# One expert's layer-1 weights copied per tile instead of its whole record, layer 2 addressed by a register of TensorE, seven places for returning rows, half 1's scatters in two of three steps

## The reference, cut to what matters

```python
def step(state, bc):                     # 512 in a row, state 64 wide
    b_t, c_t = bc
    s = _layernorm(state @ A_bar + b_t, ln_st_g, ln_st_b)
    return (s, c_t * s)
...
logits = xn @ moe_gate_w + moe_gate_b
topw, topi = jax.lax.top_k(logits, K)    # 2 of 8 experts for each token
topw = jax.nn.softmax(topw, axis=-1)
...
h  = _gelu(jnp.einsum('bsd,edh->ebsh', xn, ew1) + eb1[:, None, None, :])   # layer 1: 128 -> 256
eo = jnp.einsum('ebsh,ehd->ebsd', h, ew2) + eb2[:, None, None, :]          # layer 2: 256 -> 128
moe_out = jnp.einsum('ebsd,bse->bsd', eo, w_dense)
for i in range(NROT):
    moe_out = moe_out @ expm(gens[i])
...
x = x + s * g
```

## Time and profile before

| | us |
|---|---|
| runs, median of 3 | 410.24 (409.66 to 414.73) |
| the profiled execution | 405.85, its span 404.0 |
| PE busy in the span | 327.0 (81%) |
| DVE busy | 284.0 (70%) |
| ACT busy | 195.2 (48%) |
| POOL busy | 188.8 (47%) |
| DMA moved | 54.81 MB, 136 GB/s |

### The profile page before, as it was taken

One profiled execution on the slowest core, in us unless ns is written; L12 is line 12 of the kernel. 1 busy time (PEld: TensorE's weight loads), 2 busy tenths in 40 slices (PEclk: granted clock), 3 DMA queues, 4 the chain that ended last, 5 costly groups with the idle time before them and its releaser, 6 DMA issues.

```text
span 404.0 us, 11723 instructions
## 1 busy us (share of the span) xinstructions
PE 327.0 (81%) x4029; PEld 244.4 (60%) x4029; DVE 284.0 (70%) x1357; ACT 195.2 (48%) x587; POOL 188.8 (47%) x261
## 2 busy tenths in 40 slices
PE   2897983997787569996997999999997989887670
PEld 1676941775564347875865877877866765443340
DVE  2547589869877547876553666689999567799970
ACT  1217730201322326673636676587775573587510
POOL 8408950725546437777777545345544251000110
PEclk9999986799989959999898999899999899999955
DMA  8199950411110345665564668866656222600001
GB/s 255 22 190 163 135 117 0 130 35 36 41 40 29 140 123 187 231 222 184 189 195 158 219 192 261 280 215 203 210 178 219 79 92 56 228 28 27 28 29 55
DMA packets 44158, 54.81 MB, mean 136 GB/s; under 512 B 6840, under 2 KB 28767, under 8 KB 44095
## 3 DMA queue, kind: packets, MB, share of 16 engines
q1 hardware_dynamic: 38975, 42.52, 37.7%
q0 software_dynamic: 4544, 9.39, 7.1%
q10 hardware_dynamic: 576, 2.10, 1.5%
HBM read 14.15 MB, written 16.63 MB: 76 GB/s over the span
## 4 chain that ended last, share of the span: by engine, by line
PE 40%; DVE 32%; POOL 8%; issue 8%; DMA 6%; ACT 2%; SPq 2%; POOLq 0%; DVEq 0%; ACTq 0%
PE bank L1478 8%; PE bank L1047 7%; PE bank L1488 5%; DVE wT L949 4%; DVE ring L961 3%; DVE roots L914 3%; DMA token_rows<-rows_out,token_rows_i 3%; DVE sqj L938 2%; PE bank L465 2%; PE bank L492 2%; POOL sorted_rows L1701 2%; POOL late L307 2%; DVE xpad L1254 2%; DVE Rho L916 2%; PE bank L1471 2%
## 5 line engine op out<-in xcount | busy, mean ns | idle before, releaser
L1715 POOL DMA_INDIRECT token_rows<-rows_out,token_rows_i x78 | 75.8, 972 | 71.9 <-ACT rows_out L1612 47.6
L1701 POOL DMA_INDIRECT sorted_rows<-late,slots x64 | 63.8, 997 | 56.6 <-PE bank L1047 34.3
L1047 PE MATMUL bank<-Mrep,wT 32*32 32x64 f32 x2368 | 65.9, 226 | 18.8 <-DVE wT L949 18.0
L1047 PEld LDWEIGHTS bank<-Mrep,wT 32*32 32x32 f32 x2368 | 42.2, 108 | 52.6 <-issue 49.3
L1605 ACT ACTIVATE desk<-bank,record 128x128 f32<-128x128 f32 x156 | 48.9, 366 | 36.1 <-PE bank L1478 35.6
L961 DVE SCALAR_TENSOR_TENSOR ring<-bank,Rho,Dv 128x64 f32<-128x64 f32 x112 | 31.6, 282 | 40.5 <-PE bank L1047 38.6
L1478 PE MATMUL bank<-desk,record 128*128 128x128 f32 x312 | 58.5, 313 | 0.0
L1488 PE MATMUL bank<-record,desk 128*128 128x129 f32 x312 | 50.2, 285 | 0.0
L1478 PEld LDWEIGHTS bank<-desk,record 128*128 128x128 f32 x312 | 43.1, 200 | 7.5 <-issue 1.0
L1488 PEld LDWEIGHTS bank<-record,desk 128*128 128x128 f32 x312 | 43.2, 201 | 0.1
L1597 ACT ACTIVATE desk<-bank,cols 128x128 f32<-128x128 f32 x78 | 36.0, 462 | 6.4 <-PE bank L1471 6.4
(11 more groups left out here) (328 smaller groups left out, 658.8 us busy)
## 6 DMA issues: line engine op xcount, KB each, us to landing
record<-experts SPq DMA_DIRECT2D x78, 290.5 KB
sorted_rows<-zero_rows SPq DMA_DIRECT2D x2, 2515.5 KB, 26.6
desk<-sorted_rows SPq DMA_DIRECT2D x26, 193.5 KB
pulls<-token_rows SPq DMA_DIRECT2D x8, 516.0 KB, 5.2
X<-in_L_attn_x ACTq DMA_DIRECT2D x4, 512.0 KB, 5.5
out<-xT SPq DMA_DIRECT2D x8, 256.0 KB, 2.0
token_rows<-rows_out,token_rows_i POOLq DMA_INDIRECT x78
experts<-in_L_ffn_ew SPq DMA_DIRECT2D x1, 1024.0 KB, 28.1
```

The lines of the kernel that those rows point to most:

```text
L1047: t = pe.matmul(psY[q], wT[q, 32 * c:32 * c + 32], Mrep[q, c, :], start=(c == 0), stop=(c == 1))
L1701: pool.indirect_dma_start(sorted_rows[h], bass.IndirectOffsetOnAxis(ap=slots[:, j, q:q + 1], axis=0), sort_rows[:, q, :], None)\
L1715: pool.indirect_dma_start(token_rows[h], bass.IndirectOffsetOnAxis(ap=token_rows_i[:, g:g + 1], axis=0), rows_out[:, g % OUT_PLACES, :], N ...
```

## The change

The buffers of whole records become `first_w`, five buffers of layer 1's 256 floats a partition (`FIRSTS` = 5), free again when `layer1` of five tiles before is done. Layer 2's weights and its bias are no longer copied: PE reads the tile's expert number into a register itself (`expert_now`, at the end of the slot before) and its three layer-2 operands are addressed in `experts` by it. Layer 1's bias comes from `tile_bias`, which one matmul with a one-hot table makes for all tiles at t = 13 (two more parts of `tile_tables` on DVE at t = 10 and 11, one ACT copy); a transpose and a copy in the front are gone. SP no longer waits for the bias part; PE does, before slot 3. `rows_out` has 7 places. From t = 24 on a scatter stands only in steps that three doesn't divide.

```diff
-RECORDS = 5
-OUT_PLACES = 5
+FIRSTS = 5
+OUT_PLACES = 7
@@ tile_tables
+            elif part == 10:
+                dve.tensor_scalar(one_expert[:, 2, :], expert_f[0:E * K, :, :].rearrange("p h t -> p (h t)"), float(K), slot_at[0:E * K, 0, 0:1],
+                                  ALU.mult, ALU.subtract).then_inc(sem("tables"), 1)
+            elif part == 11:
+                dve.wait_ge(sem("tables"), 11)
+                for k in range(K):
+                    t = dve.tensor_scalar(one_expert[:, k, :], one_expert[:, 2, :], float(-k), None, ALU.is_equal)
+                t.then_inc(sem("tables"), 1)
@@ the tables of steps
+        SCATTER_AT = {}
+        for t in range(STEPS):
+            if SCATTER_LEAD + len(SCATTER_AT) < 4 * Q and (t < 2 * Q - SCATTER_LEAD or t % 3):
+                SCATTER_AT[t] = SCATTER_LEAD + len(SCATTER_AT)
@@ TensorE
+                def expert_now(g):
+                    expert[g] = pe.value_load(expert_of[0:1, g:g + 1], min_val=0, max_val=E - 1)
+
                 def layer1(g):
-                    w, _, _, _ = record_of(g)
-                    pe.wait_ge(sem(f"record{g % RECORDS}"), 16 * (g // RECORDS + 1))
+                    w = first_w[:, g % FIRSTS]
+                    pe.wait_ge(sem(f"first_w{g % FIRSTS}"), 16 * (g // FIRSTS + 1))
...
                 def layer2(g):
-                    _, w, _, bias = record_of(g)
+                    _, w, _, bias = fields(experts[:, ds(expert.pop(g), 1), :].squeeze(1))
...
                     if t in SLOT_AT:
                         j = SLOT_AT[t]
+                        if j == 2:
+                            expert_now(0)
+                        if j == 3:
+                            pe.wait_ge(sem("eb2_stored"), 32)
+                            pe.wait_ge(sem("ew2r_ready"), E)
...
                         if j >= 3:
                             layer2(j - 3)
+                        if 2 <= j < TILES + 1:
+                            expert_now(j - 1)
@@ GpSimd
-                    if SCATTER_LEAD + t < 4 * Q:
+                    if t in SCATTER_AT:
                         pool.wait_ge(sem("product"), turn)
-                        scatter(SCATTER_LEAD + t)
+                        scatter(SCATTER_AT[t])
@@ SyncE
-                    if g >= RECORDS:
-                        sp.wait_ge(sem("rows_done"), g - RECORDS + 1)
-                    sp.dma_start(record[:, g % RECORDS], experts[:, ds(e, 1), :].squeeze(1)).then_inc(sem(f"record{g % RECORDS}"), 16)
+                    if g >= FIRSTS:
+                        sp.wait_ge(sem("pre_hidden"), g - FIRSTS + 1)
+                    sp.dma_start(first_w[:, g % FIRSTS], experts[:, ds(e, 1), 0:F].squeeze(1)).then_inc(sem(f"first_w{g % FIRSTS}"), 16)
...
                 sp.wait_ge(sem("ew1_loaded"), 16)
-                sp.wait_ge(sem("ew2r_ready"), E)
-                sp.wait_ge(sem("eb2_stored"), 32)
```

More of the change, by code:

```diff
@@ L219, in build @@
         mean, var, r1, rz, nm1, nmz, tmp, tmp2 = (lnv[:, i, :] for i in range(8))
-        records = record[:, :, :].rearrange("p a r -> p (a r)")
-        lg, oh1, oh2, rest = (records[:, i * NS * E:(i + 1) * NS * E].rearrange("p (q e) -> p q e", e=E) for i in range(4))
-        hits, places = (records[:, i * NS * E:(i + 2) * NS * E].rearrange("p (e j q) -> p e j q", e=E, j=2) for i in (4, 6))
+        lg, oh1, oh2, rest = (scratch[:, i * NS * E:(i + 1) * NS * E].rearrange("p (q e) -> p q e", e=E) for i in range(4))
+        hits, places = (scratch[:, i * NS * E:(i + 2) * NS * E].rearrange("p (e j q) -> p e j q", e=E, j=2) for i in (4, 6))
         counts = sb("counts", [P, 4, HALVES, E])
@@ L1181, in out_bank @@
             return banks[3 + g % 2][:, 0:W]
-        def record_of(g):
-            return fields(record[:, g % RECORDS])
         def value_steps(n):
@@ L1520, in _ @@
                         ew2_rotation(EW2_ROT_AT[t] + 1)
+                    if t == TILE_BIAS_AT:
+                        pe.wait_ge(sem("tables"), 12)
+                        pe.matmul(banks[5][:, 0:K * TILES], eb1_rows[:, :], one_expert[:, 0:K, :].rearrange("p k t -> p (k t)"), start=True, stop=True)\
+                          .then_inc(sem("tables"), 1)
                     if t == EB2_AT:
+                        pe.wait_ge(sem("tile_bias"), 1)
                         pe.matmul(banks[5][0:E, 0:W], eb2T[:, :], Rall[:, :], start=True, stop=True).then_inc(sem("eb2_rotated"), 1)
@@ L1599, in gelus @@
                 def gelus(g):
-                    _, _, bias, _ = record_of(g)
                     act.wait_ge(sem("pre_hidden"), g + 1)
+                    if g == 0:
+                        act.wait_ge(sem("tile_bias"), 1)
                     if g >= 2:
@@ L1604, in gelus @@
                     for k in range(K):
-                        t = act.activation(hidden[:, g % 2, k, :], hidden_bank(g)[:, k * P:(k + 1) * P], ACT.Gelu, bias=bias[:, k:k + 1])
+                        t = act.activation(hidden[:, g % 2, k, :], hidden_bank(g)[:, k * P:(k + 1) * P], ACT.Gelu, bias=tile_bias[:, k, g:g + 1])
                     t.then_inc(sem("hidden"), 1)
@@ L1625, in _ @@
                         rotated_copy(EW2_ROT_AT[t] + 1)
+                    if t == TILE_BIAS_AT:
+                        act.wait_ge(sem("tables"), 13)
+                        act.copy(tile_bias[:, :, :], banks[5][:, 0:K * TILES].rearrange("p (k t) -> p k t", k=K)).then_inc(sem("tile_bias"), 1)
                     if t == EB2_AT:
@@ L1783, in _ @@
                 for g in range(TILES):
-                    if g + RECORDS < TILES:
-                        fetch(g + RECORDS)
+                    if g + FIRSTS < TILES:
+                        fetch(g + FIRSTS)
                     if g % CHUNK == 0 and g // CHUNK + 3 < TILES // CHUNK:
```

17 lines of the change are left out of this document (10 added, 7 removed).

## The result

The changed kernel takes 418.54 us in the median of 4 runs (416.94 to 421.14), the kernel before beside it 409.95 us (405.63 to 414.73). The ratio is 1.029, its 95% interval 1.024 to 1.035 (it leaves disturbed runs out, so it is not quite the quotient of the medians). So the change makes the kernel **slower by about 3%**. The forecast of 413.0 us was 5.5 us too low. The time lies inside the range of 404 to 422, but beyond the "within 2%" to which I had given the largest chance.

What follows compares the result with a forecast made beforehand. POOL was taken as the bound of the stage from 153.5 to 211.0 us. Gate -1.0 (start included), clock +2.0 and registers +2.0 sum to +3.0 us; shifted onto the median of 410.24 this gives 413, range 404 to 422.

Steps and rivals of the forecast that it cites:

- the time of the gate: Step 73: last scatter starts at 227.8, layer 1 of tile 36 at 233.6, 1.0 us earlier than before (-3.5 to +3).
- Before step 73 POOL hides it all: Slots ahead of step 73: PE's register work costs nothing there, being hidden behind POOL.
- POOL's 60 operations: From the first `rows_back` at 150.6 to the last scatter: 60 x 1.278 = 76.7 us, plus gaps, ending at 227.8.
- 0.5 us of gaps: POOL ahead of the last scatter: idle time before its lag has built up, 0.5 us in all.
- rival 3: Gate at step 73 opens later (slow landing, POOL idling or late fetches): 4 to 6 us more, 417 to 420; chance 0.13.
- The start: Front of the kernel: SP starts 1.5 us earlier without the bias wait; the first rows come 1.4 us earlier in sum.
- The clock: Steps after the stall at step 73: PE at a lower clock costs 2.0 us (bounds 0.5 and 3).
- The registers: Some 40 slots behind step 73: PE's register work for layer 2 costs 2.0 us (bounds 0 and about 8).
- short by about 0.1: Steady slot step on PE: 1.1 us of added sequencer time against 1.14 us of room, some 0.1 for waits.
- Copies of 128 KB: Weight fetches of 128 KB instead of 290.5: no wait there is for a record, so fewer bytes alone save nothing.
- The first (scatters early enough): Step 73: POOL at 1.16 us an operation, so no stall; 403, down to 399 us; chance 0.10.
- The second (register work dear): Slot steps: tight ones short by 0.5, 40 steps at 0.3 more, 12 us: 425, times 418 to 430; chance 0.20.

Runs made afterwards that it cites:

- fixed address: The changed kernel without PE's register read, layer 2 reading expert g modulo 8 at a fixed address (wrong expert for most tiles): 411.46 us, ratio 1.013.
- whole records: The kernel before with seven places and half 1's scatters in two of three steps, copies still of 290.5 KB: 412.71 us, ratio 1.013.

## Why the prediction was right or wrong

**The mechanism and the place were right.** POOL was the bound from 153 us on. The change sets one stall at step 73, for the fetched weights, with all engines standing, and the chain through scatter, load and fetch is as foretold. ACT's waits are gone. The direction was right; the size was 5.5 us short in the median and 12 in the profiled execution.

**The step that failed most is the time of the gate, and in it "Before step 73 POOL hides it all"**. The prediction has "layer 1 of tile 36 starts at 233.6"; it started at 241.57. Behind the last scatter the sum was right to 0.1 us: foretold 227.8 to 233.6, 5.8 us, measured 235.70 to 241.57, 5.87 (landing 2.37 for 2.4, spacing 1.18 for 1.4, the fetch 2.25 for 2.0). The 7.9 us lie ahead of it, in two terms.

- *POOL's 60 operations*: 77.2 us foretold, 155.26 to 235.70, 80.4, measured. The rate was right, 0.30 us of gap behind an operation of 0.96, but "0.5 us of gaps" was 3.2 short. Two waits right behind the first `rows_back` are POOL idling before its lag has built up, as rival 3 had it. The largest gap is at a round's boundary; kernel after:

```profile
198.45 0.96 POOL L1732 DMA_INDIRECT sorted_rows<-late,slots  x1 [2.82 <-PE bank L1055]
```

  and the same place in the kernel without the register, with the same schedule:

```profile
187.54 0.99 POOL L1732 DMA_INDIRECT sorted_rows<-late,slots  x1 [0.16 <-issue]
```

  A scatter waits for its step's product, and a boundary step takes over 4 us. With register work POOL had caught up by then and stood 2.8 us. Without it, in both kernels with this schedule (fixed address, and whole records), POOL has lag enough to ride over the boundary, and the 60 operations take 78.9 and 78.4 us. The likely reason is the pace ahead of it: steps 28 to 50 take 42.3 us after, 40.7 and 40.2 in those two. So of the 3.2 us some 1.6 to 2.0 are the register work, which the prediction held to be hidden ahead of the gate, and the rest are the first waits. It is read from one profile of each kernel.

- *The start*: first `rows_back` at 150.6 foretold, 155.26 measured. As a term of the change it was right. In the run without register whose front is that of before, SP's first read comes 1.48 us earlier (foretold 1.5), and in the three profiled runs with that front steps 0 to 27 take 57.1 to 57.5 us against 58.8 before. The first `rows_back` of one of them, the fixed-address kernel, starts at 151.07, close to the foretold 150.6. The profiled run of after differs in two things that other kernels share: its step 0 starts 1.3 us later, and its steps 20 to 25 run into half clock at 126 to 136 us (15.38 us instead of 11.92), most of which the stall at step 27 gives back (4.2 instead of 7.1 us). Seven places alone on the kernel before has both too. So I count this part of the 12 us as the profiled runs' difference; that no part of it is the change's isn't shown, with one profile of each kernel. It is also why a sum against one execution can't be better than some 4 us here.

**The clock** after the stall: 2.0 us foretold, the shift grows from 7.0 at the gate to 8.9 at step 76, 1.8. The rows of the first stall were the right measure. The half-clock stretch is from 238.9 to 245.7 us. A last one near 380 us cost 1.7 more, which I had not in the sum; runs of other kernels have it in some cases and not in others.

**The registers** were mis-sized: 2.0 foretold, all of it behind the stall, with bounds of 0 and 8, and 6.5 measured by the ratios. Behind the stall the changed kernel's trace has 4.7 us more than before, but not all of it is register work: 2.8 lie in the 36 steps from 76 to 114 that run at full clock in both traces, and 1.9 in three steps that a half-clock stretch touches, which is twice as long after as before. Windows of step starts over these two stretches, after and then before:

```profile
262.80:269.60 6.80, 0.49 (x2) 0.50 0.89 294
...
254.00:257.40 3.40, 0.49 (x2) 0.50 1.00 361
```

The other 1.6 to 2.0 us of register work stand ahead of the gate, as said. The kind of argument was right, an excess over the room of 1.14 us. The failing number was "short by about 0.1": it is 0.3, as one slot of after shows: ACT's copy ends at 224.50, and the next step's first weight load is 1.46 us on, 0.48 of it waiting for issue.

```profile
225.96 0.29 PEld L1055 LDWEIGHTS bank<-Mrep,wT 32*32 32x32 f32 x16 [0.48 <-issue]
```

I had put the three address instructions at 0.09 us each with their gaps; they come 0.13 us apart, and they stand ahead of the matmuls that should cover the read. The read itself, of PE in the kernel after (min, median, max in ns):

```profile
L1486 PEldq TENSOR_LOAD <-expert_of x78: 297/306/570, 149.2 to 343.9; - x78
```

Its median of 0.306 us lies near SP's 0.274 and not at PE's single 0.488 of the earlier trace rows. The Trainium skill's page "DMA: Bandwidth & Descriptors" (latency and other measured facts) gives a `tensor_load` about 600 ns at least; these 78 disagree, and with its figure the forecast would have been nearer the time for a wrong reason.

**Copies of 128 KB**: "fewer bytes save nothing by themselves" held for the stall (9.4 us with whole records, 8.9 and 7.0 with layer 1 alone) and at step 67. Between two of the experiments some 0.8% is unexplained (above), and may be theirs; with the two-in-three schedule nothing is.

**The rivals.** The first (scatters early enough) did not come. The second (register work dear) came in part. The third (a later gate) came, by POOL's gaps and not by the landings that I had named for it. I gave them 0.20 and 0.13 as if apart, but part of the later gate is the register work itself. As large as they came, each alone stays within 2%, and both together pass it. The chance of "slower", 0.28, should have been nearer a half, since my own sum lay at +3 and every open term pointed upward.

## What to carry to other kernels

When a queue is the bound, count its operations up to the one that a later engine waits for, not those per step: thinning them out relieves the steps and makes the last one late. More buffers are the cheap cure for a backlog that ends by itself; starting the queue's work earlier won as much. A wait that hides other work hides it only while it lasts: here the register work cost 1.6% beside the stall and 2.9% without it, and it delayed the very operation that was to hide it. Register work on TensorE's sequencer cost little up to what the queued matmuls cover and then, in this kernel, up to 0.41 of each 0.65 us added, so measure the room first. Here it was cheaper behind the largest group of queued matmuls than ahead of a transpose on which ACT waits.

## What the hardware showed that I had not expected

- The cost of sequencer work on PE isn't proportional: in the profiled runs 0.15 us more (the read alone) costs nothing, the next 0.25 us (the addresses) 0.07 a slot, the next 0.65 us (a second read) 0.41 a slot. The times of the runs leave up to 1.2% for the first.
- A matmul whose address comes from a register takes its 0.275 us as before; ahead of it stands one instruction of the sequencer, 0.05 us long and 0.13 us to the next.
- Stretches at half clock also come without a stall of PE (in the changed kernel it was busy 5.14 of the 6.70 us ahead of the stretch at 126 us). Of the 14 profiled executions (the two kernels and twelve experiments) ten have one from about 127 us on, whatever the edit; these are the ones whose step 0 starts at 88.1 to 89.4 us, and the four that start at 87.4 to 87.9 have none there. It takes 2.7 to 5.1 us more in steps 20 to 25, partly given back at step 27. The late front has a clock stretch ahead of it: in nine of the ten the half-clock stretch that begins at 51 to 54 us lasts 6.8 us, in the four it lasts 3.4 (51.2 to 58.0 after, 52.6 to 56.0 before); the tenth, of the disturbed group, has another pattern. What sets its length isn't shown.
- One whole group of runs, the kernel before among them, was 11% slower than on the same chip earlier, while in its one profile the instructions are as long as in the trace with one unused read (DVE 284.0 us busy against 284.1, POOL 188.9 against 188.5), apart from more steps at half clock. The cause isn't in the trace.
